# GNN kernel on one core: build slots led by a wide one, transposes at the end of a half, a compact compare table, and two last stages multiplied in the first pass

## The reference

```python
def sage_conv(x, src, dst, W_l, b_l, W_r, n_nodes):
    agg = segment_sum(x[src], dst); cnt = segment_sum(ones, dst)
    return (agg / max(cnt, 1)) @ W_l.T + b_l + x @ W_r.T
# L0: relu(sage_conv(x)), then sage_conv again
# L1, three times, with batch norm and relu between:
m = concat([x[dst_f], x[src_f], ea_f], axis=1) @ W.T + b
agg = segment_sum(m, dst_f); return relu(agg)
# x = layernorm(x + L0(x)); x = layernorm(x + L1(x))
```

## Time and profile before

| | us |
|---|---|
| median of 3 runs | 1252.13 (1249.96 to 1257.56) |
| the profiled execution | 1251.87 |
| its span, first to last instruction | 1250.0 |
| PE busy | 1066.4 |
| DVE busy | 750.7 |
| ACT busy | 347.2 |
| POOL busy | 106.2 |

### The profile page before, as it was taken

How to read it: one execution, slowest core, us unless ns; L and a number is a source line. 1 busy time by engine, 2 the same in 40 slices (tenths; PEclk the granted TensorE clock), 3 DMA queues, 4 the chain that set the end, 5 groups by cost and what they waited for, 6 DMA issues and landing times. The chain is left out here.

```text
span 1250.0 us, 21716 instructions
## 1 busy us (share of the span) xinstructions
PE 1066.4 (85%) x8748; PEld 662.0 (53%) x8748; DVE 750.7 (60%) x1480; ACT 347.2 (28%) x651; POOL 106.2 (8%) x127
## 2 busy tenths in 40 slices
PE   0255888789999979699999999999789998899993
PEld 0245888778888969444555544444334443344442
DVE  5799999898878673352433475445465546323344
ACT  1534555545565543010000001101411103300000
POOL 3111122211121101100000000000000000000001
PEclk9976788778888889789999999999889998999997
DMA  5222444345555542789277533765205765016650
GB/s 151 52 65 62 157 131 162 111 159 168 164 161 159 184 139 117 236 348 326 106 275 312 205 158 127 300 234 218 110 22 215 270 266 233 14 73 270 255 222 21
DMA packets 66976, 217.41 MB, mean 174 GB/s; under 512 B 31904, under 2 KB 44827, under 8 KB 53203
## 3 DMA queue, kind: packets, MB, share of 16 engines
q1 hardware_dynamic: 58756, 164.74, 37.5%
q0 software_dynamic: 8112, 51.21, 10.9%
HBM read 170.92 MB, written 45.00 MB: 173 GB/s over the span
## 5 line engine op out<-in xcount | busy, mean ns | idle before, releaser
L1201 PE MATMUL PM<-Aring,Xop 128*128 128x512 fp8e4 (+1 forms) x1960 | 398.5, 363 | 0.0
L1201 PEld LDWEIGHTS PM<-Aring,Xop 128*128 128x128 f16 x1960 | 181.3, 98 | 216.8 <-issue 16.3
L1201 PE MATMUL PM<-Ares,Xop 128*128 128x512 fp8e4 x588 | 136.1, 386 | 2.2 <-ACT Xop L1745 1.4
L1706 ACT ACTIVATE F<-PH,bag 64x512 f32<-64x512 f32 (+1 forms) x39 | 25.5, 658 | 381.8 <-PE PH L1419 381.7
L684 PE MATMUL PW<-key,lo 128*128 128x52 fp8e4 (+2 forms) x2466 | 117.9, 211 | 0.7 <-ACT F L746 0.2
L684 PEld LDWEIGHTS PW<-key,lo 128*128 128x128 fp8e4 x2466 | 114.7, 104 | 3.6 <-ACT F L746 1.1
L697 PE MATMUL PA<-Ares,ea 128*128 128x32 f16 x1867 | 111.5, 234 | 0.0
L1540 DVE TENSOR_SCALAR S<-PM 128x256 f32<-128x256 f32 (+1 forms) x75 | 31.3, 418 | 130.1 <-PE PM L1201 118.4
L634 PE MATMUL PT<-ident,Ares 128*128 128x128 f32 x32 | 10.8, 438 | 114.7 <-ACT Ares L712 114.7
L697 PEld LDWEIGHTS PA<-Ares,ea 128*128 128x128 f16 x1867 | 107.6, 115 | 0.0
L1201 PEld LDWEIGHTS PM<-Ares,Xop 128*128 128x128 f16 x588 | 55.8, 99 | 72.0 <-issue 9.0
(11 more groups left out here) (144 smaller groups left out, 1151.8 us busy)
## 6 DMA issues: line engine op xcount, KB each, us to landing
Aring<-adj SPq DMA_DIRECT2D x72, 1568.0 KB, 9.9
adj<-Xop POOLq DMA_DIRECT2D x12, 1568.0 KB, 5.5
adj<-stage POOLq DMA_DIRECT2D x12, 1568.0 KB, 5.9
Ares<-adj SPq DMA_DIRECT2D x6, 1568.0 KB, 22.3
rc<-ea_sum SPq DMA_DIRECT2D x36, 128.0 KB, 5.8
eaf<-in_erow SPq DMA_DIRECT2D x62, 51.0 KB
Aring<-adj SPq DMA_DIRECT2D x4, 784.0 KB, 4.3
s<-Ares POOLq DMA_DIRECT2D x24, 128.0 KB, 3.0
```

Of the source, the lines that this page charges most:

```text
L1201: last = nc.tensor.matmul(o, x[:, h, :], rhs, start=h == 0, stop=h == NT - 1)
L1706: nc.scalar.activation(F[0:64, c:c + w], PH[b % 2][0:64, 0:w], ACT.Relu, bias=t["bag"][:, 4 + conv:5 + conv]).then_inc(s_hr, 1)
```

## The change

1. Slots (`led`): in each window one slot is moved to the front, and may be widened (up to three quads, or its own width), so that fewer later slots are cut. `cuts` is now computed from the set of quads already started. By the plan's own lists, matmuls of slots go from 2466 to 2151, and their columns from 209,040 to 210,236; in halves 16 to 30 there are 109 matmuls fewer, in the others 206.
2. `turn(t + 3)` moves on PE from the start of an even half to its end, behind the attribute sums. `table(t + 3)` moves on ACT from the even iteration, where it stood behind `natural`, to the next odd one, behind `evacuate`.
3. `H` is compared with a table of its own, `iv`, 26 x 2 numbers side by side, loaded with one more DMA ahead of two others.
4. Stages 23 and 24 are not multiplied in the build. `remaining` does it on PE at the start of pass 0, out of the stage buffers into `PM`. `lo`, `key` and `stage[1]` move into `Aring`, which is now allocated before the build. DVE's `sums` takes the last three quarter blocks from `PM`. SP's last `reciprocals`, DVE's first `rest` and the last `sums` wait for a new semaphore `s_fin`.

```diff
+def led(w):
+    slots = [(j, qa, width) for j, (qa, width) in enumerate(w)]
+    low, high = min(qa for _, qa, _ in slots), max(qa + width for _, qa, width in slots)
+    options = []
+    for j, qa, width in slots:
+        for a in range(max(low, qa + width - max(3, width)), qa + 1):
+            for e in range(qa + width, min(a + max(3, width), high) + 1):
+                new = [(j, a, e - a)] + [x for x in slots if x[0] != j]
+                options.append((53 * parts(new) + 20 * (e - a - width), new))
+    return min(options, key=lambda o: o[0])[1]
...
-SLOT = [(x // 4, j, qa, width, j == 0, j == len(w) - 1) for x, y, w in WINDOWS for j, (qa, width) in enumerate(w)]
+SLOT = [(x // 4, j, qa, width, i == 0, i == len(w) - 1)
+        for x, y, w in WINDOWS for i, (j, qa, width) in enumerate(led(w))]
...
+EARLIER = NST - 2
...
+        kept.append(m["Aring"][:, :, :, :].rearrange("p i s c -> p (i s c)")[:, 0:3 * NT * SW])
...
+        iv = within(0, [128, 26, 2], i16)
...
-        lo = sb("lo", [128, 2, HS, 64], u16)
-        key = sb("key", [128, 2 * QW], u16)
+        lo = within(3, [128, 2, HS, 64], u16)
+        key = within(3, [128, 2 * QW], u16)
...
+        def multiplied_after(h):
+            return [st for st in unpacked_after(h) if st < EARLIER]
...
+            sp.dma_start(iv[:], ins["c_iv"].rearrange("p (a b) -> p a b", b=2)).then_inc(s_io, 16)
...
                 nc.vector.tensor_tensor(
-                    H[:, t % 2], io[:, 16:42, 0:2].rearrange("p v (o e) -> p o v e", o=1).broadcast_to(shape),
+                    H[:, t % 2], iv[:].rearrange("p v (o e) -> p o v e", o=1).broadcast_to(shape),
                     d[:, 2].rearrange("p (q o e) -> p q o e", o=1, e=2).broadcast_to(shape), ALU.is_equal)
...
             for h in range(NH):
-                if h % 2 == 0 and h // 2 + 3 < TS:
-                    turn(h // 2 + 3)
-                for st in unpacked_after(h - 1) if h else []:
+                for st in multiplied_after(h - 1) if h else []:
                     product(st)
...
                     if start:
-                        seen = qa
-                    cuts = [(y, z) for y, z in ((qa, min(seen, qa + w)), (max(seen, qa), qa + w)) if y < z]
-                    seen = max(seen, qa + w)
+                        seen = set()
+                    cuts = runs(qa, w, seen)
+                    seen |= set(range(qa, qa + w))
...
                     last.then_inc(s_pp, 1)
+                if h % 2 == 0 and h // 2 + 3 < TS:
+                    turn(h // 2 + 3)
...
                 if h % 2 == 0 and h // 2 + 3 < TS:
                     natural(h // 2 + 3)
+                if h % 2 and h // 2 + 3 < TS:
                     table(h // 2 + 3)
...
+            sp.wait_ge(t["s_fin"], 1)
             reciprocals(2)
...
+        def remaining():
+
+            for st in range(EARLIER, NST):
+                n, b = stage_width(st), st // 2
+                of = (t["Aring"][:, 1, 1, :] if st % 2 else m["Xop"][1][:].rearrange("p a b -> p (a b)").bitcast(f8))
+                of = of[:, 0:NT * n].rearrange("p (h d) -> p h d", h=NT)
+                for h in range(NT):
+                    last = nc.tensor.matmul(PM[b % 2][:, st % 2 * SW:st % 2 * SW + n], Xop[:, h, :], of[:, h, :],
+                                            start=h == 0, stop=h == NT - 1)
+                last.then_inc(t["s_fin"], 1)
...
+        if fused:
+            remaining()
...
+                    stored = fused and c + h < EARLIER * SW
+                    of = by_quad(sraw[:, c + h:c + h + w] if stored else PM[b % 2][:, h:h + w])
```

More of the change, by code:

```diff
@@ L61, with runs, parts @@
 WINDOWS = [w for a in range(0, NP, BANK) for w in cut(a, a + BANK)]
-SLOT = [(x // 4, j, qa, width, j == 0, j == len(w) - 1) for x, y, w in WINDOWS for j, (qa, width) in enumerate(w)]
+def runs(qa, width, seen):
+    found = []
+    for q in range(qa, qa + width):
+        if found and (q in seen) == (q - 1 in seen):
+            found[-1][1] = q + 1
+        else:
+            found.append([q, q + 1])
+    return found
+def parts(slots):
+    n, seen = 0, set()
+    for _, qa, width in slots:
+        n += len(runs(qa, width, seen))
+        seen |= set(range(qa, qa + width))
+    return n
+def led(w):
[10 more added lines that the diff above has]
+        for x, y, w in WINDOWS for i, (j, qa, width) in enumerate(led(w))]
 NS = len(SLOT)
@@ L221, in sem @@
             return ctx.enter_context(nc.semaphore(name))
-        taken = [0] * RB
+        kept = [m["Ares"][:, i].rearrange("p s c -> p (s c)") for i in range(RB)]
+        kept.append(m["Aring"][:, :, :, :].rearrange("p i s c -> p (i s c)")[:, 0:3 * NT * SW])
+        taken = [0] * len(kept)
         def within(i, shape, dt):
@@ L229, in within @@
             taken[i] = at + -(-size // 32) * 32
[L230 to L231 removed]
+            assert taken[i] <= kept[i].shape[1]
+            x = kept[i][0:shape[0], at:at + size].bitcast(dt)
             names = "abcde"[:len(shape) - 1]
@@ L436, in _ @@
                     keep(st)
-                for st in unpacked_after(h - 1) if h >= 1 else []:
+                for st in multiplied_after(h - 1) if h >= 1 else []:
                     keep_product(st)
@@ L588, in _ @@
             first(3)
-            v.wait_ge(s_io, 48)
+            v.wait_ge(s_io, 64)
             digits(0)
@@ L700, in _ @@
                     last.then_inc(s_pp, 1)
+                if h % 2 == 0 and h // 2 + 3 < TS:
+                    turn(h // 2 + 3)
             for h in (NH - 1, NH):
-                for st in unpacked_after(h):
+                for st in multiplied_after(h):
                     product(st)
@@ L779, in _ @@
                         high(c)
-                for st in unpacked_after(h - 2) if h >= 2 else []:
+                for st in multiplied_after(h - 2) if h >= 2 else []:
                     take(st)
@@ L849, in layers @@
             "s_rb": [sem(f"s_rb{i}") for i in range(len(FACTORS))],
+            "s_fin": sem("s_fin"),
             "s_xp": [sem(f"s_xp{i}") for i in range(len(GIVEN))],
@@ L1262, in products @@
         def products(i):
-            b0, b1 = SUMS[i]
             c0, c1 = reach(SUMS[i])
+            c1 = min(EARLIER * SW, c1)
             for z in range(2):
-                sp.wait_ge(m["s_so"][z], 16 * len(range(z, min(NST, 2 * b1), 2)))
+                sp.wait_ge(m["s_so"][z], 16 * len(range(z, c1 // SW, 2)))
             sp.dma_start(sraw[:, c0:c1], m["s0"][:, c0:c1]).then_inc(t["s_sr"][i], 16)
@@ L1466, in _ @@
             if p in (0, 1) and i == NB and not slow:
-                if p == 1:
-                    pe.wait_ge(s_S, NB)
-                else:
+                pe.wait_ge(s_S, NB)
+                if p == 0:
                     landed(pe, 0)
@@ L1521, in sums @@
                     v.wait_ge(t["s_rb"][piece_of(FACTORS, b)], 16)
+                    if 2 * b + 1 >= EARLIER:
+                        v.wait_ge(t["s_fin"], NST - EARLIER)
                 else:
@@ L1819 @@
     arr["c_io"] = np.tile(np.repeat(np.concatenate(steps).astype(np.int16), 16), (128, 1))
+    arr["c_iv"] = np.tile(np.repeat(steps[2].astype(np.int16), 2), (128, 1))
     arr["c_iop"] = np.tile(np.repeat(np.arange(PD, dtype=np.int16), 2), (128, 1))
```

6 lines of the change are left out of this document (3 added, 3 removed).

## The result

The changed kernel takes 1205.36 us (median of 4 runs, 1199.79 to 1208.97); against the kernel before, run beside it (median of 4 runs 1254.31), the ratio is 0.9608, with a 95% interval of 0.9554 to 0.9662.

A forecast was written before the change was run, and what follows sets the result against it. DVE was taken to set the pace from 56 to 260 us, PE to 437, then single waits to 515. Terms 14.1 + 3.3 + 1.5 + 6.0 + 0 + 6.0 = 30.9 us off 1251.87 gave 1221.0 us, range 1206 to 1237.

The forecast's parts named there:

- the seam: Passage from build to pass 0: with two products moved out, pass 0 starts at 508.9 instead of 514.9 us, 6.0 us.
- The move of the turn: PE's turn and ACT's table in the build: 3.3 and 1.5 us in DVE's stretch, 6.0 us in PE's.
- PE's early start: Build, 56 to 260 us: DVE is 94% busy, so PE starting early at even halves was said to shorten nothing.
- the clock: PE's clock, called the one resource that can't be summed; kept as it was, though one product takes 5.53 or 7.20 us.
- The compact table: Compare of H (L518): 3.175 to 1.88 us, 16 times; 14.1 us in all, none of it from five in PE's stretch.
- The strict reading of the rule: Compare of H: full rate needs runs of two adjacent 4-byte words; the repeated digit keeps it slow, 1235 us, chance 0.06.
- Fewer matmuls: Slots: bound by columns, so 315 fewer matmuls give 0; bounds 0.5 us lost or 5.2 us gained.
- Turns and tables, in DVE's stretch: 56 to 260 us: three DVE waits for eax 1.1 us shorter each, 3.3 us; one pair of evacuation waits, 1.5 us.
- Turns in PE's stretch: 260 to 437 us: four turns no longer wait, 1.22 to 2.06 us of idle each, 6.0 us together.
- Rival A: PE's stretch: with the gaps gone the clock rises, twelve products at 5.53 us, some 15 us more: 1206 us, chance 0.12.
- The moved products: Products 23 and 24, into pass 0's wait for the transposed input: 6.0 us, bounds 2 to 9 us.
- rival E: ACT's table in the odd iteration waits up to 4.5 us, 13 times; all exposed 58 us lost, 1279 us, chance 0.03.

The follow-up runs named there:

- a_slow_table: The changed kernel with the compare of H reading the old table again (two numbers of every sixteen): 1220.18 us.
- a_every_quad: The changed kernel with every slot but the first of a window cut into matmuls of one quad each, 3466 instead of 2151: 1206.28 us.
- a_turn_back: The changed kernel with PE's turn and ACT's table back at the start of the even half: 1235.85 us.
- a_turn_only_back: The changed kernel with only PE's turn back at the start of the even half, ACT's table copy staying in the odd iteration: 1230.45 us.
- b_table: The kernel before with the compact table alone: 1236.98 us.
- a_back_filled: The kernel of a_turn_back with 12 more matmuls of 256 columns, result unused, ahead of each turn from half 8 on: 1221.26 us.
- b_turn: The kernel before with turn and table moved alone: 1229.47 us.
- a_filled: The changed kernel with 12 more matmuls of 256 columns, result unused, ahead of each turn from half 8 on: 1208.07 us.
- a_interleaved: The changed kernel with one ACT take moved ahead of across, plus a half's attribute sums issued between the next product's matmuls: 1203.69 us.

## Why the prediction was wrong

The direction was right, and so were the table, the slots and the seam within some 3 us. The move of the turn was not: forecast at 10.8 us, it gives 23 us alone and costs 30.5 us when undone, more than the table, which the forecast had first. Two steps failed in it, the worth of PE's early start (15.2 us forecast up to product 5, 24.1 measured) and the clock (6.0 forecast in PE's stretch, 16.0 measured). By the steps:

*The compact table* (14.1 us): right. 1.884 us an operation; undone it costs 14.8, alone it gives 15.4. Undone, 4.2 us of that fall in PE's stretch, which I had put at 0. The strict reading of the rule in the Trainium skill (Vector Engine (DVE) Microarchitecture Reference, section 5.2, "The SBUF access granule: adjacent pairs") falls: with the digit still a single 4-byte word that is repeated, the compare takes 1.884 us, and with the table's words 32 bytes apart (a_slow_table) it takes 3.199 us.

*Fewer matmuls* (0): right, and by a_every_quad 1315 more cost 2.4 ns each. The Trainium skill (TensorE: Matmul & The Clock Gate, "Back-to-back issue gap") gives some 81 ns for a weight load and matmul at 128 columns. The slots don't show it: a_every_quad's 3466 take 122.0 us, 35 ns each with 61 columns on the mean.

*Turns and tables, in DVE's stretch* (3.3 + 1.5 us): this term was too small. 24.1 us were gained there against 15.2. The step that failed is "where DVE is 94% busy, letting PE start early shortens nothing". It shortens nothing while DVE sets the pace, but it is cashed once, at the hand-over. The trace before:

```profile
255.80 0.97 DVE L557 TENSOR_SCALAR Xop<-F 128x3136 uint16<-128x3136 uint16 x1
...
260.76 1.49 PE L656 MATMUL PX<-stage,Xop 128*128 128x256 fp8e4 x6
```

and the trace after:

```profile
234.47 1.88 PE L702 MATMUL PX<-Aring,Xop 128*128 128x256 fp8e4 x8
...
236.46 0.97 DVE L603 TENSOR_SCALAR Xop<-F 128x3136 uint16<-128x3136 uint16 x1
```

PE's product 5 started 5.0 us behind DVE's unpacking of stage 6 and now starts 2.0 us ahead of it. DVE's own work is 19.3 us earlier there (I had 17.6), and PE follows it 7.0 us closer. That is the wait through `small`, `across` and `natural` that I had booked as worthless. The runs bear it out. In each kernel whose turn stands at the start of the half (before, a_turn_back, a_turn_only_back, b_table, a_back_filled) product 5 starts 4.95 to 4.99 us behind that unpacking. With the turn at the end it starts 0.6 to 6.5 us ahead of it (b_turn 4.65), but for a_filled, where the fillers leave it 0.9 us behind. And b_turn, the move alone, brings product 5 forward by 17.4 us, where I had 4.8 for the move up to there.

*Turns in PE's stretch* (6.0 us): the gaps were sized right. The failed step is "PE's clock ... I keep it as it was". The stretch gained 16.0 us: 6.0 of gaps and 10.4 of products (85.5 to 75.1 us), less 0.4. Rival A was this, at 0.12; the products gave two thirds of its 15 us. That its 1206 us lie so near 1205.36 is luck: the rest came from the early start, which A didn't have. I had a product at the high clock, 5.53 us, and one that was partly at the low clock, 7.20 us (granted clock 0.76), in the earlier trace rows, and should have widened the range by them further and given A more.

*The moved products* (6.0 us): 4.9 in the trace of the whole change, 8.6 when undone. Pass 0 began 3.4 us after product 22 instead of 10.3, so 6.9 were gained at the seam. Then two things gave back: product 23 ran at the low clock in part (granted clock 0.67, 7.99 instead of 5.51 us), and SP's second batch of loads was late, as the start of pass 0 shows:

```profile
463.86 0.35 SPq L1322 DMA_DIRECT2D Aring<-rc_d  x1
...
470.28 0.33 SPq L1337 DMA_DIRECT2D cnt<-ea_sum  x1
```

```profile
464.58 7.99 PE L1513 MATMUL PM<-Aring,Xop 128*128 128x256 fp8e4 x49
...
475.15 1.08 PE L1452 MATMUL PH<-S,wl 128*128 128x512 f32 x2
...
485.88 2.05 PE L1452 MATMUL PH<-S,wl 128*128 128x512 f32 x2 [5.40 <-issue]
```

The first `post` comes 11.3 us after SP's first load (8.6 before), right behind the moved products; the third 22.0 (20.6 before), so 1.4 of the 6.9 us are gone by then. SP issues `cnt` 6.4 us after its first load (1.5 before): ahead of it SP waits 4.7 us for the stores of the attribute sums, which are issued at 463.6 to 464.6 us, as pass 0 begins. That small store is late next for SP, and I hadn't looked for it. The row doesn't name what the third `post` waits for ("issue"), and no experiment took the store away, so what it costs isn't shown.

*ACT as the bound* (rival E): the wait was real, 37.3 us and up to 5.3 us at a time, and hidden.

What stays open is the clock. Shown: unused dense work ahead of a product makes the product faster, with and without a gap (a_back_filled, a_filled), but lowers the slow time of the whole stretch only where there were gaps; the move of the turn brings the twelve from 86.4 to 75.1 us beside the other parts, and alone it brings them only to 84.2, with almost no gaps. Why the same loop without gaps runs near 7.0 us a product in b_turn and near 6.3 in the changed kernel, no single part tells: with the slots, the table or the two moved products undone one by one the twelve stay at 75.0 to 79.0 us. One part was never undone at all. `lo`, `key` and `stage[1]` lie in `Aring` in every kernel built on the changed one, and at their old place in b_turn and b_table. It isn't enough by itself, since a_turn_back has it too and takes 86.4 us, but whether the move of the turn needs it, or the slots and moved products together, no run shows. How the low stretches fall against the loop's rhythm isn't shown either.

## What to carry to other kernels

An early start of an engine that is not the bound is worth nothing now and something at the next hand-over: where another engine takes over the pace, add the distance by which it can follow more closely. When the same work shows different durations in the trace, as the products here with 5.5 and 7.2 us, the clock is a term of the sum; price it from rows of both kinds, and let the range reach the better one. Count columns, not matmuls, before merging matmuls; and in an in-order queue, look for the finished task that stands behind one that waits.

## What was not expected of the hardware

- Work added to an engine that is 96% busy can shorten the run: 12 unused matmuls a round, 14.6 us less (a_back_filled). Where there were no gaps, it only moved the slow time (a_filled).
- Cutting slots into 1315 more matmuls with their own fp8 weight loads cost 3.2 us of PE's busy time, 2.4 ns each, and nothing that the time shows, where columns per matmul fall to 52.
- A matmul of 32 columns with its f16 weight load costs as much between matmuls of 256 columns as among its like: 0.17 us a pair, 57 ns more than the 113 ns of the wide one alone (a_interleaved). Whether its own weight load is what shows, or that of the wide matmul behind it, the trace doesn't tell.
- A 16-bit compare whose table is read in single 4-byte words 32 bytes apart runs at 0.95 ns an element; with the words side by side the whole operation takes 1.884 instead of 3.175 us (0.57 ns an element).
